# Two weight matrices cast to bfloat16 in HBM during an earlier stage, and loaded from there

## The reference, cut to what matters

```python
# one core: x [2048, 2048], 16 heads of 128
def layernorm(x): return (x - mean(x)) / sqrt(var(x) + 1e-5)

xc = layernorm(x)
q, kv = heads(xc @ W_q.T), heads(xc @ W_kv.T)
qf, kvf = unit(fft(q)), unit(fft(kv))
kvf = cumsum(kvf, axis=sequence)
attn = ifft(qf * kvf).real @ W_o.T
x1 = x + layernorm(attn)

n = layernorm(x1)
base = n @ W.T + b
gates = softmax(top2(n @ gate_w.T + gate_b))
delta = sum over the 2 chosen experts of gate * (n @ A_e.T) @ B_e.T
out = x1 + layernorm(base + delta)
```

## Time and profile before

| what | us |
|---|---|
| median of 2 runs | 1683.08 (1681.21 to 1684.96) |
| the profiled execution's own time | 1683.73 |
| its span (slowest core, core 2) | 1682.2 |
| the fastest core's span (core 0) | 1667.8 |
| idle time of POOL ahead of the first `wot` load | 392.2 |
| waits of TensorE for `wot` loads, four together | 38.8 |

### The profile page before, as it was taken

How to read it: one execution, slowest core, us unless ns; L and a number is a source line. 1 busy time by engine, 2 the same in 40 slices (tenths; PEclk the granted TensorE clock), 3 DMA queues, 4 the chain that set the end, 5 groups by cost and what they waited for, 6 DMA issues and landing times. The chain is left out here.

```text
span 1682.2 us, 15335 instructions; the slowest of 8 cores (1667.8 to 1682.2 us)
## 1 busy us (share of the span) xinstructions
PE 1292.3 (77%) x5664; PEld 537.3 (32%) x5664; DVE 698.6 (42%) x977; ACT 444.5 (26%) x442; POOL 81.0 (5%) x154
## 2 busy tenths in 40 slices
PE   3479999979999966665666437999945888898885
PEld 2334444424444421111111112444423344344432
DVE  3500000000000037999999902444433555455553
ACT  3401111110110126666666500000002233323322
POOL 1100000000000000000000020111110000000000
PEclk9999999989999986666666658999977988988897
DMA  6522212121211200000000086554441221221221
GB/s 105 100 38 38 38 25 38 26 36 27 38 28 35 38 1 2 1 0 1 0 0 0 1 127 129 119 113 113 113 93 46 75 67 48 75 75 48 66 76 50
DMA packets 21777, 86.20 MB, mean 51 GB/s; under 512 B 2864, under 2 KB 3000, under 8 KB 19656
## 3 DMA queue, kind: packets, MB, share of 16 engines
q0 software_dynamic: 21088, 84.99, 23.3%
q1 hardware_dynamic: 616, 0.23, 0.1%
HBM read 111.46 MB, written 25.17 MB: 81 GB/s over the span
## 5 line engine op out<-in xcount | busy, mean ns | idle before, releaser
L308 PE MATMUL PMAIN<-AR,OV 128*128 128x512 bf16 x2048 | 460.1, 384 | 36.9 <-ACT AR L334 13.6
L308 PEld LDWEIGHTS PMAIN<-AR,OV 128*128 128x128 bf16 x2048 | 197.6, 98 | 299.9 <-issue 76.9
L347 DVE TENSOR_TENSOR OV<-AR 128x2048 bf16<-128x2048 bf16 x32 | 39.2, 1226 | 493.1 <-ACT AR L337 493.1
L842 PE MATMUL PAUX<-AR 128*128 128x512 bf16 x1024 | 235.4, 393 | 0.0
L571 PE MATMUL PMAIN<-AR 128*128 128x512 bf16 x512 | 121.0, 400 | 38.8 <-DMA AR<-wot 38.8
L418 ACT ACTIVATE AR<-PAUX 128x1024 bf16<-128x1024 f32 x128 | 124.0, 1021 | 74.9 <-DVE AR L498 42.6
L334 ACT ACTIVATE AR<-PMAIN 128x1024 bf16<-128x1024 f32 x32 | 32.7, 1023 | 415.8 <-PE PMAIN L308 415.8
L842 PEld LDWEIGHTS PAUX<-AR 128*128 128x128 bf16 x1024 | 101.6, 101 | 127.6 <-issue 15.5
L571 PE MATMUL PAUX<-AR 128*128 128x512 bf16 x512 | 111.8, 379 | 0.0
L465 PE MATMUL PAUX<-AR,MSIN 128*128 128x512 bf16 x128 | 56.3, 560 | 54.7 <-ACT AR L418 54.7
L571 PEld LDWEIGHTS PMAIN<-AR 128*128 128x128 bf16 x512 | 51.8, 102 | 107.3 <-issue 52.9
(11 more groups left out here) (114 smaller groups left out, 1135.7 us busy)
## 6 DMA issues: line engine op xcount, KB each, us to landing
AR<-x POOLq DMA_DIRECT2D x32, 512.0 KB, 5.4
out<-AR POOLq DMA_DIRECT2D x16, 1024.0 KB, 5.1
OV<-wqs POOLq DMA_DIRECT2D x16, 512.0 KB, 5.1
OV<-wkvs POOLq DMA_DIRECT2D x16, 512.0 KB, 5.1
AR<-wot POOLq DMA_DIRECT2D x16, 512.0 KB, 27.5
x1s<-AR POOLq DMA_DIRECT2D x16, 512.0 KB, 3.0
AR<-wt POOLq DMA_DIRECT2D x16, 512.0 KB, 7.1
AR<-x1s POOLq DMA_DIRECT2D x16, 512.0 KB, 6.1
```

The source lines that it names most:

```text
L308: ins = te.matmul(PMAIN[:, nn * 512:(nn + 1) * 512], lhsT, XCT[:, c * 2048 + nn * 512: c * 2048 + (nn + 1) * 512], start=(c == 0), stop=(c ...
L347: v.tensor_mul(SQ[h % 2], DEST[:, h * 2048:(h + 1) * 2048], DEST[:, h * 2048:(h + 1) * 2048]).then_inc(s_sq, 1)
L842: te.matmul(PAUX[:, nn * 512:(nn + 1) * 512], lhsT, WTB[:, c * 2048 + nn * 512: c * 2048 + (nn + 1) * 512], start=(c == 0), stop=False)
```

## The change

The program gets two more tensors in HBM, `wotb_s` and `wtb_s`, both bfloat16. In block b2 POOL gets a program: 16 DMAs from `wot` to `wotb_s` and 16 from `wt` to `wtb_s`, each 128 rows, HBM to HBM with the cast on the way. In block c POOL waits for all 32 (semaphore `s_pcast`) before the first load, and all loads of `WOTB` and `WTB` in c and d read the bfloat16 tensors, now without a cast. Everything else is as before. The diff, cut to its core:

```diff
+    wotb_d = nc.dram_tensor("wotb_s", [D, D], BF16, kind="Internal")
+    wtb_d = nc.dram_tensor("wtb_s", [D, D], BF16, kind="Internal")
...
+        @blk.gpsimd
+        def _(g):
+            for c in range(NCH):
+                g.dma_start(wotb_d.ap()[c * 128:(c + 1) * 128, :],
+                            wot_d.ap()[c * 128:(c + 1) * 128, :]
+                            ).then_inc(s_pcast, 16)
+            for c in range(NCH):
+                g.dma_start(wtb_d.ap()[c * 128:(c + 1) * 128, :],
+                            wt_d.ap()[c * 128:(c + 1) * 128, :]
+                            ).then_inc(s_pcast, 16)
...
     with nc.Block("c") as blk:
         @blk.gpsimd
         def _(g):
+            g.wait_ge(s_pcast, 16 * 2 * NCH)
             for c in range(NCH):
                 g.dma_start(WOTB[:, c * 2048:(c + 1) * 2048],
-                            wot_d.ap()[c * 128:(c + 1) * 128, :]
+                            wotb_d.ap()[c * 128:(c + 1) * 128, :]
                             ).then_inc(s_wog[c // 4], 16)
...
                 if t < NCH - 2:
                     g.dma_start(WTB[:, t * 2048:(t + 1) * 2048],
-                                wt_d.ap()[t * 128:(t + 1) * 128, :]
+                                wtb_d.ap()[t * 128:(t + 1) * 128, :]
                                 ).then_inc(s_wt, 16)
...
             for c in (NCH - 2, NCH - 1):
                 g.dma_start(WTB[:, c * 2048:(c + 1) * 2048],
-                            wt_d.ap()[c * 128:(c + 1) * 128, :]
+                            wtb_d.ap()[c * 128:(c + 1) * 128, :]
                             ).then_inc(s_wt, 16)
```

More of the change, by code:

```diff
@@ L186, in build_nc @@
     s_gmm = sm("s_gmm"); s_xamm = sm("s_xamm"); s_gprod = sm("s_gprod")
-    s_qkm = sm("s_qkm")
+    s_qkm = sm("s_qkm"); s_pcast = sm("s_pcast")
     s_gate1 = sm("s_gate1"); s_gate2 = sm("s_gate2")
```

## The result

The ratio of the changed kernel to the one before is 0.9837, with a 95% interval of 0.9825 to 0.9849. I forecast 25.8 us. Some executions of the changed kernel were disturbed on one die, so its plain median (1696.53) isn't used; the ratio compares undisturbed runs. The profiled execution took 1652.77 us, with a span of 1651.2.

A forecast was written before the change was run, and what follows sets the result against it. TensorE was near full in the weight stages but waited 38.8 us for `wot` loads at the start of c. The sum was 1683.73 - 23.0 - 2.8 = 1657.9, forecast 1658 us, own range 1647 to 1664, 8 in 10 1650 to 1677.

The forecast's parts named there:

- (1): Start of c, tile 0: sixteen `wot` loads at 1.6 us instead of 3.0 let it end earlier, 23.0 us saved.
- (2): Rounds of c: fourteen `wt` loads halve their DMA time, but are already hidden under busy PE: 0.
- (3): Start of d: the last two `wt` loads, queued ahead of the `x1s` load, get cheaper, 2.8 us saved.
- (4): b2: the 32 added HBM to HBM casts need 96 to 147 us and stay hidden: 0.
- (5): Before c's loads: POOL's added wait for the casts is long met when b2 ends: 0.
- Rival A: End of b2: casts not done, at 16 us each POOL waits 169 us, total 1827; chance 0.07.
- Rival B: Load bursts: bfloat16 loads on all eight cores are no faster than casts, total 1683; chance 0.07.
- (6): b2: disturbance by a later SELS load and POOL's issuing beside DVE, taken as 0, upper end 17 us.

The follow-up runs named there:

- e5: Against the changed kernel: no scratch tensors; `wot` loads, still casting, go straight to SBUF during b2, `wt` casts on load; ratio to before 0.9738.
- e1: Changed kernel with only `wot` cast ahead in b2; `wt` is loaded as float32 with its cast, as before; ratio to before 0.9845.
- e2: Changed kernel with only `wt` cast ahead in b2; `wot` is loaded as float32 with its cast, as before; ratio to before 0.9982.
- e4: Changed kernel with POOL holding the 32 casts back until late in b2 (head 11 of 16); one run, 1699.34 us.
- e3: Changed kernel with all 32 casts moved from b2 to b1kv, behind the strip loads; ratio to before 0.9835.
- e9: Changed kernel with the two `x1s` loads first at the start of d, ahead of `wt` and `bbt`; ratio to before 0.9801.
- e8: e5 with the two `x1s` loads first at the start of d, ahead of `wt` and `bbt`; ratio to before 0.968.

## Why the prediction was right

It was right in its sign, its size and its place: 27.4 us measured, 25.8 forecast.

(1) Tile 0: forecast 23.0, measured 26.0 on the profiled core and 63.1 - 37.5 = 25.6 by the medians. The price of a load was right, 1.58 us against 1.6. Two parts of the term were sized a little too long. The lag before the first group was 10.8 - 4 x 1.58 = 4.5 us and not 6.1, and the last group ran at the high clock throughout (3.4 us, I had 4.4). I had called 3.0 us the price of a casting load "alone or in a burst". As a pace it is that of two neighbouring cores in a burst together, as all cores mostly are here; a core whose neighbour is idle lands one each 2.5 us (last section). The start and the stop of PE were as argued; e5 shows that the arrival of weights was what bound the tile, since with the weights there T0 loses another 17.8 us.

(2) The 14 `wt` loads of c: 0, as said; e1 shows it.

(3) The start of d: 2.8 forecast, 4.6 on the profiled core, 2.1 by the medians, 2.4 and 2.5 by e1 and e2 against their counterparts. Right within the scatter of the cores. The errors of (1) and (3) go opposite ways, 2.6 us too little and 0.7 too much by the medians, so a little of the agreement is luck.

(4), (5) The casts: hidden. 149 us, just above the 96 to 147 that I had, with the read and the write both to be paid. The estimate of 162 us from the copy rate in the Trainium skill ("DMA: Bandwidth & Descriptors", section on latency and other measured facts) was near as well, though that rate is of copies without a cast. Rival A lies a factor of 2.3 away, and e4 reached it by starting late. Rival B falls: the same 512 KB written cost half when half is read and nothing is cast.

(6) The zero for b2: SELS cost 0.3 to 0.45 us on four cores, and nothing on the others. It landed 1.5 us later on the profiled core, and the slack of 1.2 us took up most of it. POOL's 15 us of issuing cost DVE nothing: 297.20 us of DVE in the changed kernel, 297.23 in e3, 297.25 in e4. The lock that the Trainium skill describes did not bind here, as the exception in the same page ("SBUF — State Buffer", section on who interferes with whom) has it for a DVE instruction with two inputs in SBUF against a GpSimd instruction that only writes; e4 agrees.

## What to carry to other kernels

In a burst of loads behind a barrier, look at the bytes that each load reads and not only at those it writes: here half the bytes read took the load from 3.0 to 1.58 us, and loads that start before the barrier took tile 0's wait away altogether (e5). Before moving a cast to scratch memory, look for SBUF that the stage before gives back head by head, since e5 took 44 us off where the change took 27, with none of the traffic. And read what stands in the queue ahead of the one load that everyone waits for: its place in the order was worth 6 us in e9 and 8 to 10 us in e8.

## What the runs showed that I had not expected

Neighbouring cores disturb each other. The delay of SELS comes from the other core's casts, as the table and e3 show. And the pace of a burst depends on whether the neighbour is in a burst too. The first two rows are core 0 before, which begins its casting loads at 966.25 while core 1 begins at 973.88. The other two are core 3 of the changed kernel, which begins its bfloat16 loads at 967.00 while core 2 begins at 972.75. The last column is GB/s written, the one ahead of it the DMA share.

```profile
969.00:974.00 5.00, 0.00 (x0) 0.00 (x0) 0.00 (x0) 0.00 (x0) 5.00 (x10) 0.50 1.05 207
980.00:1010.00 30.00, 15.84 (x42) 5.64 (x42) 0.00 (x0) 0.00 (x0) 0.00 (x0) 0.67 1.03 164
```

```profile
969.00:973.00 4.00, 0.00 (x0) 0.00 (x0) 0.00 (x0) 0.00 (x0) 4.00 (x9) 0.50 1.02 401
979.00:991.00 12.00, 9.66 (x35) 3.78 (x34) 0.00 (x0) 0.00 (x0) 0.00 (x0) 0.81 0.99 323
```

Alone a casting load takes 0.524 / 0.207 = 2.5 us and a bfloat16 load 1.3; together 3.2 and 1.6. The DMA share is full either way, so it doesn't tell a pace set by the core's own engines from one set by something shared. The casts from HBM to HBM show it most. On core 3 the second and third land 2.5 and 2.7 us after the one before, the third at 634.7, when core 2, which issues its first at 630.1, has had none land (the first does at 638.2). From the fourth to the last they are 4.7 us apart on average. On core 2 the last three are 2.4 to 2.5 us apart, once core 3's last has landed at 771.2. In e4 the last cast of the later core of each pair lands 2.4 to 2.8 us after the one before it, that of the earlier core 4.2 to 4.4 us.

So the pace of the bursts is set by something that two cores share. With both active, a cast HBM to HBM moves 1.05 MB in and 0.52 MB out in 4.7 us, 335 GB/s for a core; a casting load 1.05 MB in 3.0 to 3.2 us, 328 to 350 GB/s; a bfloat16 load 0.52 MB in 1.58 us, 332 GB/s. The Trainium skill, "HBM Reference", section on specifications, gives two cores a common 716 GB/s, 358 for each; the three paces lie 2 to 8% below it, if bytes read from HBM and written to it are added up. That the shared thing is HBM is argued from these numbers, not shown. It would also explain why the lag before the first group and D differ from core to core, before the change by 5 and 3 us: in each pair the lag is longer on the core that begins c later.

Whether a load got cheaper by its bytes or by losing its cast, no run separates. One row speaks for the bytes. In a round of d before, the store of `out`, 1.05 MB of float32 without a cast, has the 16 engines busy for 0.77 x 4.40 = 3.4 us, no less than a casting load that reads as much:

```profile
1334.00:1338.40 4.40, 4.40 (x22) 2.04 (x21) 1.71 (x9) 1.49 (x2) 1.05 (x2) 1.00 0.77 238
```
